# One Trainium2 core, attention followed by an MLP: output weights fetched one group earlier, the first layer's weights by columns and half of them split in the row part's first batch, the first y in place

## What is computed

```python
query = seq2 + b_self                                   # 512 x 512 per batch
q, k_own = query @ Wq + bq, query @ Wk + bk             # 16 heads of 32
k_prev   = (x + b_prev) @ Wk + bk
score    = concat([q @ k_prev.T (masked by length), sum(q * k_own)]) / sqrt(32)
w        = softmax(score)
attn     = w[..., :-1] @ (x @ Wv + bv) + w[..., -1:] * (seq2 @ Wv + bv)
y        = x + attn @ Wo + bo                           # Wo 512 x 512
h        = gelu(y @ W1 + b1)                            # W1 512 x 2048
out      = y + concat([h @ W2 + b2, h @ We[expert] + be[expert]])   # 384 + 128 columns
```

## Time and profile before

| | |
|---|---|
| runs | 1852.75 us median of 3 (1849.78 to 1853.16) |
| the profiled execution's own time | 1852.25 us |
| its span (first to last instruction) | 1850.4 us |
| mean granted TensorE clock | 0.97 of full |
| PE busy | 1741.3 us, 94% |
| DVE, ACT, POOL busy | 49%, 38%, 34% |
| chain that ended last | PE 72%, SP queue 7%, issue 7%, POOL 5%, DMA 4%, DVE 4% |

### The profile page before, as it was taken

One profiled execution on the slowest core, in us unless ns is written; L12 is line 12 of the kernel. 1 busy time (PEld: TensorE's weight loads), 2 busy tenths in 40 slices (PEclk: granted clock), 3 DMA queues, 4 the chain that ended last, 5 costly groups with the idle time before them and its releaser, 6 DMA issues.

```text
span 1850.4 us, 27725 instructions
## 1 busy us (share of the span) xinstructions
PE 1741.3 (94%) x8320; PEld 1280.9 (69%) x8320; DVE 911.5 (49%) x1398; ACT 712.2 (38%) x1258; POOL 623.7 (34%) x489
## 2 busy tenths in 40 slices
PE   6999999999999999999994899999999999999997
PEld 5656656666566565665661588888888888888886
DVE  4567575775766658757576633223231323232311
ACT  3254353544544435445344432323232323333222
POOL 3177484665765748648564300000000000000000
PEclk8999999999999999999996899999999999999999
DMA  6353434424343335343335321213030302131201
GB/s 143 71 112 76 96 85 99 100 65 102 85 108 80 94 71 117 73 96 83 78 89 154 101 67 32 60 24 68 16 69 17 71 20 51 34 49 42 32 14 23
DMA packets 361052, 132.67 MB, mean 72 GB/s; under 512 B 288202, under 2 KB 328138, under 8 KB 360978
## 3 DMA queue, kind: packets, MB, share of 16 engines
q1 hardware_dynamic: 356370, 129.75, 31.9%
q10 hardware_dynamic: 4608, 2.10, 0.4%
HBM read 62.02 MB, written 18.89 MB: 44 GB/s over the span
## 4 chain that ended last, share of the span: by engine, by line
PE 72%; SPq 7%; issue 7%; POOL 5%; DMA 4%; DVE 4%; ACT 1%; POOLq 0%; DVEq 0%; ACTq 0%
PE ps_proj L1140 10%; PE ps_av L1092 6%; PE ps_av L1094 6%; PE ps_av L1093 6%; PE ps_max L1171 5%; PE ps_av L1211 5%; PE ps_proj L1092 3%; PE ps_proj L1093 3%; PE ps_proj L1094 3%; PE ps_max L1092 3%; PE ps_max L1094 3%; PE ps_max L1093 3%; PE ps_score L1094 3%; PE ps_score L1093 3%; PE ps_score L1092 3%
## 5 line engine op out<-in xcount | busy, mean ns | idle before, releaser
L647 ACT ACTIVATE p_f<-ps_score 128x512 f32<-128x512 f32 x512 | 304.4, 598 | 471.5 <-PE ps_score L1198 445.1
L839 DVE TENSOR_REDUCE m_col<-ps_max 128x1 f32<-128x512 f32 x512 | 329.1, 683 | 231.6 <-PE ps_max L1171 229.9
L542 POOL TENSOR_TENSOR p_sum<-p_sum,p_f 128x512 f32<-128x512 f32 x256 | 336.5, 1345 | 2.8 <-ACT p_f L647 2.8
L1030 DVE TENSOR_TENSOR h_lo<-h_f,h_hi 128x512 fp32r<-128x512 f32 x128 | 88.4, 691 | 478.9 <-ACT h_hi L739 478.9
L539 POOL TENSOR_TENSOR p_sum<-p_f 128x512 f32<-128x512 f32 x128 | 162.1, 1298 | 240.0 <-PE ps_av L1220 237.0
L1198 PE MATMUL ps_score<-stacks 99*128 99x512 f32 x512 | 210.1, 421 | 24.2 <-ACT p_f L647 24.1
L1171 PE MATMUL ps_max<-stacks 97*128 97x512 f32 x512 | 188.2, 435 | 41.0 <-DMA stacks<-parts 28.1
L1140 PE MATMUL ps_proj<-in_hi,w_hi 128*128 128x512 f32 x512 | 208.3, 407 | 17.7 <-POOL in_lo L547 14.3
L1140 PE MATMUL ps_proj<-in_hi,w_lo 128*128 128x512 f32 x512 | 205.7, 402 | 0.0
L1140 PE MATMUL ps_proj<-in_lo,w_hi 128*128 128x512 f32 x512 | 205.6, 402 | 0.0
L1092 PE MATMUL ps_av<-y_hi,w_hi 128*128 128x512 f32 x512 | 200.2, 391 | 5.1 <-DVE den L877 4.2
(11 more groups left out here) (126 smaller groups left out, 2644.3 us busy)
## 6 DMA issues: line engine op xcount, KB each, us to landing
stacks<-parts SPq DMA_DIRECT2D x384, 128.0 KB
raw<-in_x_dram SPq DMA_DIRECT2D x128, 64.0 KB, 2.2
raw<-in_fside_BxSxS_dram SPq DMA_DIRECT2D x128, 64.0 KB, 2.2
den<-own_scratch SPq DMA_DIRECT2D x128, 64.0 KB, 2.8
attn_scratch<-num SPq DMA_DIRECT2D x32, 256.0 KB, 3.0
a_raw<-attn_scratch SPq DMA_DIRECT2D x32, 256.0 KB, 3.6
x_raw<-in_x_dram SPq DMA_DIRECT2D x128, 64.0 KB, 2.2
we_raw<-in_L_cond_We_dram SPq DMA_DIRECT2D x32, 256.0 KB, 2.7
```

What stands on the lines that cost most here:

```text
L542: pool.tensor_tensor(p_sum[:, j], p_sum[:, j], now, ALU.add).then_inc(sum_made, 1)
L647: act.activation(p_f[:, i % FLIGHT], ps_score[i % 2][:, :], ACT.Exp, scale=SCALE).then_inc(p_made, 1)
L839: dve.tensor_reduce(m_col[:, n % C, n // C:n // C + 1], ps_max[n % 2][:, :], AX.X, ALU.max).then_inc(max_made, 1)
L1030: dve.tensor_tensor(h_lo[:, m % 2], h_f[:, :], f(h_hi[:, m % 2]), ALU.subtract).then_inc(h_lo_made, 1)
```

## The change

- `wide_at` is a list of twelve positions: Wo at positions 0 to 3 of group 2, eight W1 pieces at positions 5, 7, 10, 12, 14 of group 2 and 0, 2, 4 of group 3. Pieces 12 to 19 (`EARLY` = 12 and up) are split in rows 1 to 8 of the row part's first batch (`wide_row`). They use three buffers of `raw` and semaphores of their own.
- W1's pieces are numbered by column block first, then by rows of 128, so the first eight are the first 1024 columns.
- SP issues Wo at the end of group 1, ahead of the store; pieces 4 to 8 and 9 to 11 in group 2; 12, 13, 14 in group 3; 15 to 19 between the W2 pieces and in the first batch of rows. The residuals 1 to 3 move behind attended 3.
- The W2 pieces 6 and 7 are split in rows 9 and 10, the expert's fourth piece in row 6.
- `first_y_out` writes y over the transposed x, without the wait for a buffer; three of the four stand at positions 10, 12 and 14 of group 3 on VectorE. Behind the last group VectorE's order is y 3, low 0, numerator, low 1, denominator, low 2, low 3, reciprocals, normalization.
- TensorE waits for the W1 column block that a row needs (8, 12, 16, 20 pieces at rows 0, 4, 8, 12), for the numerator before row 0 and for the denominator before row 1.

```diff
-        WIDE_FROM = 4
-        wide_at = {(2, i): (i - WIDE_FROM,) for i in range(WIDE_FROM, TILES)}
-        wide_at.update({(3, i): (i + TILES - WIDE_FROM,) for i in range(WIDE - TILES + WIDE_FROM)})
+        EARLY = 3 * C
+        wide_at = {at: (n,) for n, at in enumerate(
+            ((2, 0), (2, 1), (2, 2), (2, 3), (2, 5), (2, 7), (2, 10), (2, 12), (2, 14), (3, 0), (3, 2), (3, 4)))}
+        wide_row = {1 + n: EARLY + n for n in range(WIDE - EARLY)}
+        w2_row = {0: 2, 1: 3, 2: 4, 3: 5, 9: 6, 10: 7}
+        first_y_at = {(3, 10): 0, (3, 12): 1, (3, 14): 2}
...
-            k, at = (n - C) // (HID // S), (n - C) % (HID // S)
+            k, at = (n - C) % C, (n - C) // C
...
-        first_y = (y_f[:, :], x_t[:, :])
+        def wide_buffer(n):
+            return raw[:, n % 4] if n < EARLY else raw[:, (n - EARLY) % 3]
...
+            def wide_late(n):
+                sp.wait_ge(wide_lo_made, n - 3 if n < EARLY + 3 else n - 2)
+                sp.dma_start(wide_buffer(n), wide_source(n)).then_inc(late_landed[(n - EARLY) % 3], DMA)
...
                     if last and g == 2:
-                        for n in range(10):
+                        for n in range(4, 9):
                             wide(n)
...
-                        for n in range(10, 14):
+                        for n in range(9, EARLY):
                             wide(n)
...
+                    if last and g == 1:
+                        for n in range(4):
+                            wide(n)
                     if last and g == 3:
-                        for n in range(14, 17):
-                            wide(n)
+                        wide_late(EARLY)
                         attended(0, 2)
+                        wide_late(EARLY + 1)
+                        wide_late(EARLY + 2)
+                        attended(0, 3)
                         residual(0, 1)
-                        wide(17)
-                        wide(18)
-                        attended(0, 3)
-                        wide(19)
                         residual(0, 2)
                         residual(0, 3)
...
-            for n in range(4, W2S):
+            for n in range(4, 6):
                 w2_piece(n)
+                wide_late(EARLY + n - 1)
             for r in range(2):
                 sp.wait_ge(attn_stored[r], DMA * C * B // 2)
+            attended(1, 0)
+            attended(1, 1)
+            w2_piece(6)
+            wide_late(WIDE - 3)
+            w2_piece(7)
...
+                    if first:
+                        expert_weights(b, 3)
+                        wide_late(WIDE - 2)
...
                     attended(b + 1, 2)
+                    if first:
+                        wide_late(WIDE - 1)
                     attended(b + 1, 3)
+                    if first:
+                        expert_weights(b + 1, 0)
...
+                            if (g, i) in first_y_at:
+                                first_y_out(first_y_at[g, i])
+
+            def first_y_out(c):
+                dve.wait_ge(o_mm, c + 1)
+                dve.wait_ge(x_made, c + 1)
+                dve.scalar_tensor_tensor(out=first_x[c], in0=first_o[c][:, :], scalar=bo_col[:, c:c + 1],
+                                         in1=first_x[c], op0=ALU.add, op1=ALU.add).then_inc(y_f_made, 1)
...
-            first_y_out(0)
-            first_y_out(1)
+            first_y_out(3)
+            y_low(0, 0, first_x[0])
             numerator(B - 1, C - 1)
-            y_low(0, 0, first_y[0])
-            first_y_out(2)
-            y_low(0, 1, first_y[1])
-            first_y_out(3)
-            y_low(0, 2, first_y[0])
-            y_low(0, 3, first_y[1])
+            y_low(0, 1, first_x[1])
             denominator(B - 1, C - 1)
+            y_low(0, 2, first_x[2])
+            y_low(0, 3, first_x[3])
...
                     hidden_low(b, m)
+                    if first and m in w2_row:
+                        w2_low(w2_row[m])
                     if first and m < 2:
-                        w2_low(2 + m)
                         expert_low(b, m + 1)
-                    if m == 4:
+                    if m == (6 if first else 4):
                         expert_low(b, 3)
-                    if first and 2 <= m < W2S - 2:
-                        w2_low(2 + m)
+                    if first and m in wide_row:
+                        wide_low(wide_row[m])
...
-            def hidden(b, m, ks):
+            def hidden(b, m, ks, first):
                 n = KH * b + m
+                if first and ks[0] == 0:
+                    if m % C == 0:
+                        pe.wait_ge(wide_lo_made, C + C * (m // C + 1))
+                    if m == 0:
+                        pe.wait_ge(num_made, C * B)
+                    if m == 1:
+                        pe.wait_ge(den_made, C * B)
...
-            pe.wait_ge(wide_lo_made, WIDE)
-            pe.wait_ge(num_made, C * B)
-            pe.wait_ge(den_made, C * B)
```

More of the change, by code:

```diff
@@ L202, in cond_resid_program @@
         attn_stored = [sem(f"attn_stored{r}") for r in range(2)]
+        late_landed = [sem(f"late_landed{i}") for i in range(3)]
         wide_landed = [sem(f"wide_landed{i}") for i in range(4)]
@@ L881, in wide_low @@
                 dve.wait_ge(wide_hi_made, n + 1)
-                dve.tensor_tensor(lo, raw[:, n % 4], f(hi), ALU.subtract).then_inc(wide_lo_made, 1)
+                dve.tensor_tensor(lo, wide_buffer(n), f(hi), ALU.subtract).then_inc(wide_lo_made, 1)
             def attended_low(b, c):
@@ L1053, in _ @@
             w2_low(1)
+            dve.wait_ge(y_lo_made, C)
             expert_low(0, 0)
@@ L1327, in outputs @@
                 mm.then_inc(out_mm, 1)
-            pe.wait_ge(wide_lo_made, WIDE)
-            pe.wait_ge(num_made, C * B)
-            pe.wait_ge(den_made, C * B)
             def rows(b, first, last):
                 for m in range(2):
-                    hidden(b, m, range(C - 1))
+                    hidden(b, m, range(C - 1), first)
                 for m in range(2):
-                    hidden(b, m, range(C - 1, C))
+                    hidden(b, m, range(C - 1, C), first)
                 residuals(b)
@@ L1341, in rows @@
                     if m + 2 < KH:
-                        hidden(b, m + 2, range(C))
+                        hidden(b, m + 2, range(C), first)
                     outputs(b, m, first)
```

42 lines of the change are left out of this document (21 added, 21 removed).

## The result

The changed kernel takes 1842.57 us, the median of 7 runs (1836.09 to 1846.12); beside it the kernel before takes 1850.55 us, also of 7 (1845.57 to 1855.21). The ratio is 0.995, with a 95% interval of 0.993 to 0.9969: faster, by 8 us in the medians and 9 by the ratio, and its whole interval lies on that side by more than the 0.2% that can be told. The forecast was 1842.0 with a range of 1835 to 1850. The profiled execution of the changed kernel took 1842.57 us with a span of 1840.8.

What follows compares the result with a forecast made beforehand. Bound: dense TensorE row part, preceded by a hole in the last attention batch's groups 2 and 3, where ScalarE waits for W1 fetches. Sum -9.0 - 2.1 + 1.3 - 0.7 = -10.5 on 1852.25: 1842.0 us, range 1835 to 1850.

Steps and rivals of the forecast that it cites:

- Part 1: Group 2, last attention batch: Wo splits at positions 0 to 3 wait for Wo; 6.7 us lost, between 5.5 and 8.
- Part 2: Group 3: eight of twelve splits gone, value burst at 1012.3 instead of 1021.34; 9.0 us won, group 2's loss included.
- Part 3: End of attention: y in place, denominator behind one y and two low parts; 2.1 us won, bounds 0 and 3.3.
- The clock charge of 1.3 us: TensorE before its third hidden block: idle some 4 us, then lower clock; 1.3 us lost, between 0 and 3.
- Part 4: Row part: eight splits moved into rows 1 to 8 cost nothing; the 0.67 us stall at 1079.60 goes, 0.7 won.
- C: Rival, slower: W1 waits in group 3 become attention-fetch waits, 29.7 us up to the burst stays; 1857 us, chance 0.09.
- D: Rival, row part: fetches of rows 4 to 8 miss the cover by 1 us each; 1847 us, chance 0.04.
- A: Rival, more: group 3's attention fetches near 3 us, burst 4 to 6 us sooner; 1837 us, chance 0.20.
- B: Rival, about nothing: group 2's later sums hold exponentials, group 3 only pays group 2; 1849 to 1851 us, chance 0.07.

Runs made afterwards that it cites:

- changed_again: The changed kernel, unedited, run and profiled a second time: 1847.34 us, ratio 0.9964 to the kernel before.
- attention_first: Changed kernel with Wo split at positions 4 to 7 of group 2, attention pieces 0 and 1 fetched and split ahead of W1's: 1835.06 us, ratio 0.9916.
- normalize_later: Changed kernel with group 2's normalization on VectorE moved from position 15 of group 3 to behind the last numerator: 1844.69 us, ratio 0.9963.

## Why the prediction was right, point by point

- **Where the time goes, and the mechanism.** Right in both directions. Group 2 got longer, group 3 shorter by more, and the waits on ScalarE are close to those forecast: 9.41 us for Wo (8 to 9 forecast), 2.58 and 3.53 for the attention result (2 to 4), none over 2 us for W1.
- **Part 1, 6.7 us lost.** The step was under-sized: 9.3 us at the own maximum in the changed kernel (36.2 against 27.0), outside its own bounds of 5.5 to 8, and 8.4 at the end of the chain. Wo took 4.7 us from issue to landing (968.90 to 973.62) where I had 3.7, so it came 1.0 us later than computed; the maxima behind it all the same ended as computed, by luck then: at 987.11, and 988.3 less the 1.4 us of origin is 986.9. The failed term is what I gave burst, denominators and own scores behind them, 3.1 us on the assumption that TensorE would have its full clock back. It had not: 3.64 us of burst, 1.80 of denominators, granted clock 0.54, 5.4 us in all.
- **Part 2, by itself.** The forecast had 15.7 us (9.0 won at the burst, with 6.7 lost in front of it). Alone it moved the burst by 15.3 and the last normalization by 16.1. The changed kernel's burst was 6.5 us sooner than before, not 9.0, by the 2.6 us that group 2 was later. In the second profile it was 5.1 us sooner: there the waits for the attention result were 3.68, 3.97 and 1.21 us instead of 2.58, 3.53 and 0.47.
- **Part 3, 2.1 us won.** 0.8 here: burst to last normalization took 28.7 us instead of 29.5. The term was a little large, 1.7 us by the means of the quiet profiles, and the rest is the long normalization of 4.23 us, which stands in front of the last y, the last low parts and the denominator (1036.88 where I had 1034.4). It was not in any case that I had weighed. In the second profile, without it, the stretch took 27.1 us: 2.4 won.
- **The clock charge of 1.3 us.** Right for the kernel, though not for the execution that was profiled first. There TensorE stood 3.70 us before its third hidden block and went on at full clock, granted 1.00 in front of the block and in it. By the Trainium skill's page "TensorE: Matmul & The Clock Gate" (HAM oscillation), which I weighed there, it should have fallen. In the ten other profiles with this idle time it did, as behind the 4.23 us of the kernel before, and in changed_again it cost 1.6 us.
- **Part 4, nothing, and 0.7 won.** Right: at full clock 0.94 us were won between the third hidden block and the first batch's result, 0.67 of them the stall that went. TensorE waited for nothing from 1055 to 1150.
- **The sum.** -10.5 was forecast. By the distances it is -7.3 - 0.94 = -8.2: 2.5 less won at the burst and 1.3 less in part 3, 1.3 for a drop of the clock that didn't come in this execution, 0.2 more in the rows. The remaining 1.4 us between the profiled runs lie in front of the change. In the second profile, with the drop and without the long normalization, part 3, the clock and the rows come out as forecast (2.4 won, and 0.7 lost where 1.3 less 0.7 is 0.6), and the whole miss stands at the burst: 5.1 won instead of 9.0, and 6.8 in all. So of 10.5 us forecast 7 to 8 came. That the median came out at 1842.57 for a forecast of 1842.0 is partly luck: the kernel before, measured beside it, took 1850.55 and not the 1852.25 from which the forecast counts.
- **Rivals.** C ("the waits only change their names") needed group 3 to keep over 26 of its 29.7 us up to the burst; it took 16.0. D fell with the row window. A didn't come: the attention chain was no faster than computed; in attention_first one sees VectorE's full queue in front of it and slow fetches in it. B's mechanism, sums that hold the exponentials, shows as a single wait of 0.53 us.

The likeliest reason that VectorE is slow in group 3 is GpSimd's additions beside it. No run took them away, so this rests on durations (0.69 us without, 1.40 to 1.76 with) and on one instruction that was moved: in normalize_later the normalization ran at 1030.14, after GpSimd's last sum at 1029.06, and took 0.68 us.

## What to carry to other kernels

Ask of a prefetch "in the stage before" where its issue stands in its queue: here sixteen copies and four fetches stood in front of it, it went out 0.5 us earlier, and its consumers, moved up by four positions, turned that into a loss of 8 us. Before moving a use forward, look when the queue will really let its fetch go. When a change moves several things, price each by itself: here one line cost half of what the rest won. And take a second profile of the kernel before calling a term wrong: the first one lacked a clock drop that ten others have, and had a long normalization that the second lacks, each worth 1.6 us.

## What the runs showed of the hardware that was not expected

- **A VectorE instruction can stand until GpSimd has finished its queue.** The normalization, two SBUF inputs and an SBUF output, takes 0.69 us with GpSimd idle and mostly 1.5 to 1.9 us beside its additions. Over fourteen profiles with 32 of them each, nine stretched: five of 4.2 to 4.4 us in group 3 of the last batch and four of 8.95 to 8.99. In all nine it ended 0.54 or 0.55 us after GpSimd's last addition of the run; in the two shown above at 1030.26 + 4.23 = 1034.49 against 1033.95, and at 975.31 against 974.76. GpSimd was not slowed meanwhile: its eight additions took 9.89 to 10.06 us in the nine, and 10.03 in normalize_later with no normalization beside them, but 10.46 to 10.94 beside a normal one in the last group. So beside a normal one both engines are slower, and beside a stretched one only VectorE is. What decides which comes is open.
- Three of the four of 8.95 to 8.99 us lie at 154, 155 and 181 us of three profiles, in code that is the same in all kernels; the fourth is the one directly in front of group 2. These three profiles reach group 2's negated maxima at 961.4, 962.4 and 966.5 us, the others at 950.8 to 957.7. This is a part of what makes runs of one kernel differ; the rest of that scatter isn't explained here.
- TensorE's clock fell in group 2 of the changed kernel, where it stood 8.28 us, and was still at 0.54 from 983.3 to 992.5, though it was hardly idle from 975.71 on (0.57 us). In front of its third hidden block 3.70 us of idle time passed without a drop in this profile, and 3.70 to 3.93 us were followed by one in the ten others.
